# A recurrent layer with a gated MLP on eight cores: the D·x term leaves the PSUM eviction on VectorE, which ScalarE takes over, and is added before the gate multiply

## The reference

```python
x = L0_attn_inputs                       # (8, 8192, 1024)
xn = layernorm(x)                        # no scale, no shift
Bu = einsum('ph,blh->blp', B_norm, xn)   # complex, B_norm = (B_re + i B_im) * exp(gamma_log)
xs = associative_scan(...)               # xs[t] = Lambda * xs[t-1] + Bu[t], complex, diagonal
s  = einsum('hp,blp->blh', C, xs).real + D * xn
g  = silu(relu(xn @ W1 + b1) @ W2 + b2)  # 1024 -> 4096 -> 1024
out = x + s * g
```

## Time and profile before

| | us |
|---|---|
| median of 2 runs | 4290.27 (4227.69 and 4352.86) |
| the profiled execution | 4095.21 |
| its span on the slowest core (core 5), first to last instruction | 4094.2 |
| spans of the eight cores | 4078.2 to 4094.2 |
| mean granted TensorE clock of the eight cores | 0.881 to 0.886 |

### The profile page before, as it was taken

One profiled execution on the slowest core, in us unless ns is written; L12 is line 12 of the kernel. 1 busy time (PEld: TensorE's weight loads), 2 busy tenths in 40 slices (PEclk: granted clock), 3 DMA queues, 4 the chain that ended last, 5 costly groups with the idle time before them and its releaser, 6 DMA issues.

```text
span 4094.2 us, 60600 instructions; the slowest of 8 cores (4078.2 to 4094.2 us)
## 1 busy us (share of the span) xinstructions
PE 3070.5 (75%) x21760; PEld 2228.9 (54%) x21760; DVE 2196.5 (54%) x3513; ACT 907.0 (22%) x1766; POOL 22.0 (1%) x46
## 2 busy tenths in 40 slices
PE   2402678796978878786977878796887878697898
PEld 1201365573837556473846556483756647384767
DVE  5770283746548284655648284655737374654611
ACT  3102122121213112221312212121312222131322
POOL 0010000000000000000000000000000000000000
PEclk9855789897989989898998989898998979899999
DMA  5865366482937557393846748393756649293777
GB/s 147 197 149 146 121 216 222 140 286 87 299 110 255 197 171 240 134 291 110 266 146 222 231 148 264 114 301 120 246 167 203 218 142 291 92 286 125 244 234 242
DMA packets 409221, 800.86 MB, mean 196 GB/s; under 512 B 50528, under 2 KB 50528, under 8 KB 406880
## 3 DMA queue, kind: packets, MB, share of 16 engines
q1 hardware_dynamic: 361184, 738.26, 56.0%
q10 hardware_dynamic: 41984, 41.95, 2.9%
q0 software_dynamic: 5760, 16.78, 2.7%
HBM read 755.01 MB, written 58.72 MB: 199 GB/s over the span
## 4 chain that ended last, share of the span: by engine, by line
PE 49%; DVE 22%; DMA 18%; issue 5%; ACT 5%; DVEq 1%; ACTq 1%; SPq 0%; POOL 0%; POOLq 0%
PE PB L745 16%; PE PA L785 10%; PE PB L785 10%; PE PB L539 7%; DMA wslot<-sc_w 5%; DMA out<-xsl 5%; DMA h<-W 3%; DMA sc_w<-h 2%; DMA xsl<-x 2%; PE PB L667 2%; DVE xsl L842 2%; PE PB L581 2%; DVE vv L686 2%; DVE vv L692 2%; DVE tmp L689 2%
## 5 line engine op out<-in xcount | busy, mean ns | idle before, releaser
L745 PE MATMUL PB<-xnf,wslot 128*128 128x256 bf16 x8192 | 961.0, 282 | 268.0 <-DVE vv L692 244.0
L745 PEld LDWEIGHTS PB<-xnf,wslot 128*128 128x128 bf16 x8192 | 825.8, 101 | 403.7 <-issue 285.0
L755 ACT ACTIVATE h<-PB,b_tab 128x256 bf16<-128x256 f32 x1024 | 485.6, 474 | 1413.8 <-PE PB L745 1286.2
L785 PE MATMUL PA<-h,wslot 128*128 128x256 bf16 x4096 | 467.9, 273 | 47.5 <-ACT h L755 42.0
L819 DVE TENSOR_TENSOR g_b<-s_b,g_b 128x1024 f32<-128x1024 f32 x64 | 78.4, 1225 | 759.2 <-ACT g_b L799 759.2
L785 PE MATMUL PB<-h,wslot 128*128 128x256 bf16 x4096 | 468.1, 273 | 0.0
L785 PEld LDWEIGHTS PA<-h,wslot 128*128 128x128 bf16 x4096 | 398.1, 98 | 102.4 <-issue 56.6
L785 PEld LDWEIGHTS PB<-h,wslot 128*128 128x128 bf16 x4096 | 400.8, 98 | 46.3
L539 PE MATMUL PB<-xsre,wslot 128*128 128x512 bf16 x1024 | 270.9, 412 | 136.1 <-DVE s_b L550 92.2
L667 PE MATMUL PA<-xnf,wslot 128*128 128x512 bf16 x1024 | 266.9, 424 | 107.7 <-DVE vv L692 107.7
L401 PE MATMUL PB<-ident,s_b 128*128 128x128 f32 x256 | 62.1, 424 | 292.0 <-ACT s_b L393 203.5
(11 more groups left out here) (84 smaller groups left out, 2468.5 us busy)
## 6 DMA issues: line engine op xcount, KB each, us to landing
wslot<-sc_w SPq DMA_DIRECT2D x256, 2048.0 KB, 11.4
wslot<-sc_b SPq DMA_DIRECT2D x32, 2048.0 KB, 11.6
wslot<-sc_c SPq DMA_DIRECT2D x32, 2048.0 KB, 11.1
xsl<-x SPq DMA_DIRECT2D x32, 1024.0 KB, 5.8
out<-xsl ACTq DMA_DIRECT2D x32, 1024.0 KB, 8.2
h<-W POOLq DMA_DIRECT2D x8, 1024.0 KB, 14.3
sc_w<-h SPq DMA_DIRECT2D x8, 1024.0 KB, 8.8
h<-W POOLq DMA_DIRECT2D x32, 256.0 KB, 4.6
```

Source lines behind the costliest of these rows:

```text
L745: inst = nc.tensor.matmul(bank[:, 0:256], pslot(jw)[:, kk * 1024 + ml * 128: kk * 1024 + (ml + 1) * 128], xnf_p[:, kk * NSUP + sub * NSUB: ...
L755: ev = S(lambda m2=mi, b=bank: nc.scalar.activation(h1[:, m2 * NSUB:(m2 + 1) * NSUB], b[:, 0:256], AF.Relu, bias=b1_tab[:, m2:m2 + 1]))
L785: inst = nc.tensor.matmul(w2bank[m], pslot(jw)[:, kl * 1024 + m * 128: kl * 1024 + (m + 1) * 128], h1[:, (q * 8 + kl) * NSUB: (q * 8 + kl ...
```

## The change

The eviction in the C stage moves from VectorE to ScalarE and becomes a plain copy of the bank into `s_b`. The product `D * xnf` is added later, in place in `s_b`, by VectorE: in each half of the MLP stage, behind the wait for the fourth Silu and ahead of the multiply, four instructions of 128x256. The wait that protects `xnf` against being overwritten (`du_last`) now names VectorE's last instruction of the half in which it was last read.

```diff
@@ C stage @@
                 last_cx = TE.inc(inst)
-                VX(TE, last_cx)
-                sev = V(lambda mm=m, b=bank:
-                        nc.vector.scalar_tensor_tensor(
-                            s_b[:, mm * NSUP:(mm + 1) * NSUP],
-                            xnf_p[:, mm * NSUP:(mm + 1) * NSUP],
-                            d_tab[:, mm:mm + 1],
-                            b,
-                            ALU.mult, ALU.add))
-                pp_release(bk, "VE", sev)
-            sevac_last = VE.n
+                SX(TE, last_cx)
+                sev = S(lambda mm=m, b=bank: nc.scalar.activation(
+                    s_b[:, mm * NSUP:(mm + 1) * NSUP], b, AF.Identity))
+                pp_release(bk, "SE", sev)
+            sevac_last = SE.n
@@ transposes @@
                     if k >= 2:
                         SX(TE, w1_last[k % 2])
-                        SX(VE, sevac_last)
+                        SX(VE, du_last[k % 2])
@@ MLP and output @@
                 for hf in range(2):
                     VX(SE, new_gev[sub][hf * 4 + 3])
+                    for mm in range(hf * 4, hf * 4 + 4):
+                        V(lambda m2=mm:
+                          nc.vector.scalar_tensor_tensor(
+                              s_b[:, m2 * NSUP + sub * NSUB:
+                                  m2 * NSUP + sub * NSUB + NSUB],
+                              xnf_p[:, m2 * NSUP + sub * NSUB:
+                                    m2 * NSUP + sub * NSUB + NSUB],
+                              d_tab[:, m2:m2 + 1],
+                              s_b[:, m2 * NSUP + sub * NSUB:
+                                  m2 * NSUP + sub * NSUB + NSUB],
+                              ALU.mult, ALU.add))
@@ end of the pass @@
             g_ev = new_gev
+            du_last[(k - 1) % 2] = VE.n
```

More of the change, by code:

```diff
@@ L260, in build_program @@
     sevac_last = 0
+    du_last = [0, 0]
     g_ev = [[0] * 8, [0] * 8]
```

## The result

The changed kernel is slower by 1.5%: the ratio of its runs to those of the kernel before is 1.0151, 95% interval 1.0117 to 1.0184. In later runs beside the experiments it was 1.0160 (1.0128 to 1.0192). The medians, 4172.4 us (11 runs) and 4172.2 us (10 runs), don't show it, because they hold slow runs (in those of the changed kernel the four cores of one die ran at a granted clock of 0.81 to 0.86 in the mean), among them the two behind the forecast's level of 4290.3 us, and the ratio leaves these out. The lowest runs are 4152.2 and 4097.1 us. The growth is under the 2% that the prediction took for the least that can be told from no change; the interval tells it from none.

A forecast was written before the change was run, and what follows sets the result against it. No engine bounds the kernel alone: a pass is a relay between engines. First halves 41, second halves 11 and ScalarE's eviction -3 give +49 us, on 4290.3 us a forecast of 4339 us, range 4140 to 4405.

The forecast's parts named there:

- the forecast's level: Base of the forecast time: the median of the two runs shown, 4290.3 us, 195 us above the profiled execution.
- Sum: Whole kernel: 41 + 11 - 3 = +49 us, 4144 us on the profiled execution, 4339 us on the median of two runs.
- clock loss: Behind TensorE's two pauses at the end of first halves: lower granted clock, 1.3 us each, 21 us over 16.
- Part 2: First halves: lateness 45.6, clock 21, less 21 of weight waits and 5 of clock losses behind them: 41 us.
- Part 1: End of each half: eight new instructions of 485 ns delay the second multiply by 2.87 or 2.52 us, 86.2 us gross.
- The waits for weights and the stores: W1 and the halves' stores: late stores shorten and land nearly on time, so 21 us of TensorE's weight waits is recovered.
- Part 3: Second halves and boundaries: stores issued 2.52 us late shorten by 2.0, leaving 0.5 us each; 11 us in all.
- The cover at the fifth chunk: C stage: TensorE's wait for evictions hides its own lateness and clock loss; the wait stays at 5 to 7 us.
- Part 4: C stage: the first ScalarE eviction comes no sooner, the last ends 0.1 us sooner; 0.2 us in 15 passes, -3 us.
- Rival 2: C stage: ScalarE evicts as soon as a chunk is ready, the 92.2 us of waits go; -43, 4247 us; chance 0.05.
- Rival 1: Stores keep their 8.2 us and give nothing back; 4373 to 4400 us, 1.9 to 2.6% slower; chance 0.22.
- rival 3: All is covered, with no clock loss and short stores; -2 to +20 us, 4288 to 4310; chance 0.11.

The follow-up runs named there:

- Experiments 4 and 10: The changed kernel with matmuls of unused result filling TensorE's pauses at each half's end: both pauses (4) 1.0073, the longer second only (10) 1.0059 to the kernel before.
- Experiment 3: The kernel before with four extra VectorE instructions between the last addition to the tokens and each half's store; 1.0027 to the kernel before.
- experiment 5: The changed kernel with the additions of D*x ahead of the Silu wait in first halves only; 0.9991 to the kernel before.
- experiment 1: The changed kernel with all eight additions of a half ahead of the Silu wait, evictions still on ScalarE; 1.0013 to the kernel before.
- experiment 7: The changed kernel with all additions ahead of the Silu wait and ScalarE's second layernorm wait moved behind the sixth eviction; 0.9723 to the kernel before.

## Why the prediction was right and wrong

The direction and the place were right: slower, by 1.5% where the sum gave 1.2% of the profiled execution, and in the first halves. Two steps failed.

The first is the level in the step "Sum". The forecast of 4339 us was set on the median of two runs, which is 193 us above the lowest run of the kernel before (4097.1), and it is 167 us over the 4172 us measured. The prediction itself says that its terms don't grow with that level; the consequence would have been to take the profiled execution's 4095 us as the base, which with +49 gives 4144, 0.7% under the measured median and 8 us under the lowest run. That 4172 us lies between 4140 and 4405 is owed to a range that was made wide enough for both levels, and says nothing of the mechanism.

The second is the clock loss of Part 2, put at 21 us (16 x 1.3) where 42 (16 x 2.65) was measured. Step by step:

- *Part 1, the delay.* Right. 256 additions of 484 ns; the second multiply starts 6.0 us after the fourth Silu (2.34 + 3.69).
- *Part 2, first halves, +41 us.* Right in kind, low in size: +63 us. I took 1.3 us per half out of a range of 0 to 1.66, the 1.66 read from 64 matmuls behind one wait. It left out that the transposes behind the pause run at half clock as well (1.94 for 1.06 us, 0.88 more) before W1 loses its own 1.77 (29.95 for 28.18): 2.65 us where no wait covers it. It also allowed for ends at which the clock stays up, and in first halves there were 2 of 128. With 2.65 in the sum: 45.6 + 16 x 2.65 - 21 - 5 = 62 us, the measured 63. Experiments 4 and 10 give 2.4 and 2.6 us per half back by keeping the clock up.
- *The waits for weights and the stores.* Right: 24.0 us of waits went to 3.7, the stores' median to 5.5 us. Experiment 3 shows that lateness alone shortens the stores; it can't show the waits for weights alone, since TensorE was late in it too.
- *Part 3, second halves, +11 us.* About right in its terms, and too high in what can be seen. I had the store give back 2.0 of 2.52 us: in the mean of eight cores the second halves' stores were issued 2.57 us later, counted from the fourth Silu, and landed 0.4 us later, so they gave back 2.1. The cover at the fifth chunk held, though with 3.7 us in the mean that wait was shorter than the 5 to 7 I had named. Yet the boundaries are 0.3 us shorter instead of 0.5 longer, and experiment 5, with the additions late in second halves only, is at -0.09% (-0.33 to +0.14), 6 us at most.
- *Part 4, ScalarE's eviction, -3 us.* Not to be told from nothing (experiment 1: +0.13%, interval -0.06 to +0.31).
- *Rival 2.* Its mechanism did not occur, for the reason given: the first eviction stood behind layernorm (the wait for L242 shown above, 14 times). Its price was about right: with the order changed (experiment 7) the boundary gives back 8.0 us, 111 us over 14 passes. This is more than the 92.2 us of waits; the fifth chunk's first eight matmuls also take 1.89 us instead of 3.57.
- *Rival 1 and rival 3.* Out: stores did shorten, and the clock did fall.

In the sums, the low end of the first halves is 20 by its own terms (45.6 - 21 - 5), not 21, and 4140 stands for 4144; nothing hangs on either.

What stays open: why the boundaries show nothing of stores that land 0.4 us later, and why the clock fell at nearly all ends of first halves and at a quarter of those of second halves.

## What to carry to other kernels

Work taken off an eviction that nobody waits for is worth nothing. The same work put between the last matmul's result and the next one's input costs its length and, on top, the clock, less what a later wait covers: in the first halves here most of it was paid, in the second halves nothing that can be seen. Price a new pause of TensorE with everything that runs slowly behind it, the short transposes included. Work that needs only old data belongs ahead of the wait, not behind it (experiment 1 costs nothing for the same arithmetic). And before moving an eviction to an idler engine, look at what stands ahead of it in either queue: here a change of order alone gave 2.6 to 2.8%, on either engine. And look at what stands behind a wait that you lengthen: in experiment 3 a late store held back ScalarE's evictions and through them TensorE.

## What the runs showed of the hardware that was not expected

- A pause of 2.62 us behind eight transposes of 1.07 us, themselves behind a pause of 1.39 us, brought the granted clock to 0.50 in the stretch behind it. In the kernel before, the one pause of 1.30 us left all transposes at full clock (274 ns in the mean); but with a second one of 1.44 us close behind it the granted clock was 0.52 from 668.4 on the earlier trace rows. And a pause of 2.05 us within W1 in experiment 3, behind 3.66 us of matmuls, left them at full clock: 202 in 22.21 us, 110 ns each, as in 28.18 us for 256. So the length of one pause doesn't decide alone. Filling the long pause with matmuls kept the transposes at 276 ns. The second pause of the kernel before:

```profile
665.94 1.06 PE L830 MATMUL PB<-ident,g_b 128*128 128x128 f32 x8 [1.30 <-DVE g_b L819]
668.44 3.45 PE L539 MATMUL PB<-xsre,wslot 128*128 128x512 bf16 x8 [1.44 <-DVE xsl L842]
```

- A 1 MB store that is issued while a 2 MB load is still under way took 8.2 us in the median, and 5.5 us when it was issued 2.3 to 2.9 us later. It landed at nearly the same time: counted from the fourth Silu, 0.2 us later in first halves and 0.4 us in second halves of the changed kernel.
